# One written-out order of pieces replaced by another on all five queues of a vision tower kernel

## What is computed

```python
h = tok(x)                     # depthwise 3x3 convolution, 8x8 mean pooling: 64 tokens an image
h = h + attn0(layernorm(h))    # one head, 128 wide; values are the normalised tokens themselves
h = h + moe(layernorm(h))      # 2 shared experts, and the best 2 of 8 routed ones; hidden width 512
h = h + attn1(layernorm(h))    # 8 heads, rotary; 64 own keys, 15 compressed keys and a sink
h = h + mlp(layernorm(h))      # two 128x128 lower-triangular products with a gelu between
```

## Time and profile before

| | |
|---|---|
| time, median of three runs | 1983.51 us |
| the profiled execution's own time | 2000.31 us |
| its span, first to last instruction | 1998.4 us |
| TensorE busy | 1700.6 us, 85% |
| VectorE busy | 1307.9 us, 65% |
| ScalarE busy | 1070.4 us, 54% |
| GpSimd busy | 754.4 us, 38% |
| mean granted TensorE clock | 0.932 of full |
| moved by transfers | 331.56 MB, 166 GB/s |

### The profile page before, as it was taken

The page is one execution under the profiler, slowest core; times in us unless marked ns, Lnnn a source line. Parts: engine busy times, 40 slices in busy tenths (PEclk is TensorE's granted clock), DMA queues, the critical chain, the costliest instruction groups (busy, mean ns, idle before and its releaser), DMA issues.

```text
span 1998.4 us, 42920 instructions
## 1 busy us (share of the span) xinstructions
PE 1700.6 (85%) x14896; PEld 1320.4 (66%) x14896; DVE 1307.9 (65%) x3244; ACT 1070.4 (54%) x2707; POOL 754.4 (38%) x643
## 2 busy tenths in 40 slices
PE   1453888989998989999899999898999999897947
PEld 1443666867677777778676777777776768575624
DVE  2467476878677777568686777777777868442222
ACT  0122545647474747466564747474757566553532
POOL 1324244352536263344525263626353434213020
PEclk9999989999899999799998999999999999988775
DMA  6547455555655554445555555555455543101000
GB/s 253 223 172 261 164 209 194 184 176 183 219 182 176 202 203 173 153 174 191 181 187 206 183 196 205 176 186 206 163 208 185 203 164 147 43 15 53 12 22 6
DMA packets 109125, 331.56 MB, mean 166 GB/s; under 512 B 13662, under 2 KB 87585, under 8 KB 92412
## 3 DMA queue, kind: packets, MB, share of 16 engines
q1 hardware_dynamic: 86416, 300.90, 41.5%
q0 software_dynamic: 8992, 19.42, 3.0%
q10 hardware_dynamic: 13516, 8.50, 1.4%
HBM read 299.48 MB, written 29.29 MB: 165 GB/s over the span
## 4 chain that ended last, share of the span: by engine, by line
PE 42%; POOL 19%; DVE 14%; issue 13%; ACT 6%; DMA 4%; ACTq 1%; another core or an unknown queue 0%; SPq 0%; POOLq 0%; DVEq 0%
PE hid_bank L595 7%; POOL yg L1374 7%; PE sec_bank L649 5%; POOL rows_d L1352 5%; PE pool_bank L449 3%; POOL xbuf L1363 3%; PE sec_bank L669 3%; PE sec_bank L660 3%; PE hid_bank L580 3%; PE hid_bank L579 3%; PE pool_bank L454 2%; DVE xc L1268 2%; POOL rs L1335 2%; DVE x L1055 2%; PE hid_bank L581 2%
## 5 line engine op out<-in xcount | busy, mean ns | idle before, releaser
L1363 POOL TENSOR_TENSOR xbuf<-xbuf 128x512 f32<-128x512 f32 x256 | 328.2, 1282 | 633.0 <-DVE xbuf L1063 621.7
L845 ACT ACTIVATE hid<-hid_bank,bias_t 128x128 f32<-128x128 f32 x960 | 273.1, 371 | 116.0 <-PE hid_bank L581 113.6
L595 PE MATMUL hid_bank<-w_s,hid 128*128 x1920 | 291.2, 297 | 0.0
L595 PEld LDWEIGHTS hid_bank<-w_s,hid 128*128 128x128 f32 x1920 | 244.4, 199 | 16.9
L1084 DVE SCALAR_TENSOR_TENSOR taps<-pooled_s,tapw,taps 128x256 f32<-128x256 f32 (+1 forms) x416 | 240.5, 578 | 10.6
L1063 DVE TENSOR_TENSOR xbuf<-xbuf 128x1536 f32<-128x1536 f32 x128 | 224.0, 1750 | 30.4 <-DMA xbuf<-in_x 30.3
L579 PE MATMUL hid_bank<-xt,w_b 128*128 128x128 bf16 x960 | 213.2, 234 | 35.0 <-issue 17.1
L580 PE MATMUL hid_bank<-xt,w_b 128*128 128x128 bf16 x960 | 213.5, 234 | 0.7
L581 PE MATMUL hid_bank<-xt,w_b 128*128 128x128 bf16 x960 | 209.5, 230 | 0.0
L1374 POOL DMA_INDIRECT yg<-outs_d,spot_i x128 | 151.2, 1182 | 54.7 <-issue 38.8
L1067 DVE TENSOR_TENSOR xbuf<-xbuf 128x512 bf16<-128x512 f32 x128 | 102.1, 797 | 98.4 <-ACT xbuf L759 94.6
(11 more groups left out here) (215 smaller groups left out, 3464.8 us busy)
## 6 DMA issues: line engine op xcount, KB each, us to landing
xbuf<-in_x SPq DMA_DIRECT2D x128, 2048.0 KB
rows_s<-rows_d SPq DMA_DIRECT2D x48, 320.0 KB, 3.4
outs_d<-ys SPq DMA_DIRECT2D x240, 64.0 KB, 7.1
out<-h ACTq DMA_DIRECT2D x16, 256.0 KB
w_s<-in_w ACTq DMA_DIRECT2D x1, 2560.0 KB
hid<-in_w POOLq DMA_DIRECT2D x10, 256.0 KB, 3.4
rows_d<-x2r,spot_i POOLq DMA_INDIRECT x128
yg<-outs_d,spot_i POOLq DMA_INDIRECT x128
```

Of the source, the lines that this page charges most:

```text
L595: mm = nc.tensor.matmul(hid_bank[n % 2][:, 0:P], hid[:, n % RING, q * P:(q + 1) * P], w_q, start=False, stop=q == FC - 1)
L845: ins = nc.scalar.activation(hid[:, n % RING, cols], hid_bank[n % 2][:, cols], ACT.Gelu, bias=bias_t[:, q, j:j + 1])
L1363: nc.gpsimd.tensor_tensor(v[:, :, 1, :], v[:, :, 1, :], v[:, :, 2 * k + 3, :], ALU.add) \
```

## The change

Only the table `ORDER` changes. Every list keeps its words; they stand in another order, and for `dve`, `sp` and `pool` some pieces at the seam between two iterations move across it, which the mark `'` shows. No instruction is added or taken away, and no wait is.

```diff
     sp="""
-        store.6' store.7' store.4' store.9' store.10' store.8' load.0.0 store.13' store.11' store.12' store.14'
-        load.0.1 rows.1 rows.0 load.1.0 load.1.1 store.1 rows.2 load.2.0 store.0 store.2 load.2.1 store.3
-        load.3.0 load.3.1 store.5 keep.0""",
+        store.9' store.5' store.7' store.11' store.8' load.0.0 store.12' store.10' store.13' load.0.1 store.14'
+        rows.0 rows.1 load.1.0 rows.2 load.1.1 load.2.0 store.1 load.2.1 store.0 store.3 store.4 store.6 load.3.0
+        store.2 load.3.1 keep.0""",
     pe="""
-        up.0 up.1 table up.2 up.3 down.0 down.1 down.2 up.4 down.3 up.5 out' up.6 down.4 down.5 up.7 pool.0.0
-        pool.0.1 down.6 down.7 pool.0.2 lift.0 att.1 lift.1 widen.0 lift.2 widen.1 att.2 narrow.0 lift.3 pool.0.3
-        lift.4 widen.2 pre.2 narrow.1 pre.3 lift.5 att.3 lift.6 narrow.2 pre.4 att.4 pre.5 pre.6 lift.7 pre.7
-        widen.3 pool.1.0 pool.1.1 widen.4 pool.1.2 score.0 score.1 att.7 score.2 score.3 narrow.3 score.4
-        pool.1.3 score.5 widen.5 narrow.4 score.6 score.7 lift.8 att.8 widen.6 narrow.5 turn.0 widen.7 turn.1
-        pool.2.0 lift.9 value.0 pool.2.1 narrow.6 turn.2 lift.10 pool.2.2 att.10 widen.8 value.1 turn.3 value.2
-        narrow.7 turn.4 pool.2.3 value.3 lift.11 widen.9 turn.5 value.4 narrow.8 turn.6 value.5 att.11 widen.10
-        turn.7 lift.12 narrow.9 value.6 narrow.10 value.7 widen.11 att.12 lift.13 post.0 widen.12 pool.3.0 post.1
-        narrow.11 pool.3.1 pool.3.2 narrow.12 lift.14 widen.13 widen.14 pool.3.3 narrow.13 post.3 narrow.14
-        post.4 post.5""",
+        up.0 table up.1 down.0 up.2 up.3 down.1 up.4 up.5 down.2 up.6 down.3 up.7 out' down.4 down.5 down.6
+        down.7 pool.0.0 lift.0 pool.0.1 widen.0 lift.1 att.1 pool.0.2 lift.2 widen.1 lift.3 att.2 pool.0.3
+        narrow.0 att.3 pre.2 widen.2 lift.4 narrow.1 pre.3 widen.3 narrow.2 att.4 pre.4 narrow.3 pre.5 pre.6
+        widen.4 lift.5 pool.1.0 pre.7 pool.1.1 pool.1.2 score.0 score.1 lift.6 att.7 widen.5 score.2 score.3
+        narrow.4 score.4 widen.6 score.5 score.6 pool.1.3 lift.7 score.7 narrow.5 narrow.6 att.8 turn.0 lift.8
+        widen.7 turn.1 value.0 lift.9 widen.8 turn.2 value.1 pool.2.0 turn.3 pool.2.1 value.2 att.10 pool.2.2
+        lift.10 turn.4 narrow.7 value.3 att.11 turn.5 lift.11 widen.9 value.4 turn.6 lift.12 value.5 pool.2.3
+        narrow.8 turn.7 narrow.9 widen.10 value.6 att.12 widen.11 narrow.10 lift.13 value.7 widen.12 post.0
+        narrow.11 lift.14 post.1 pool.3.0 widen.13 narrow.12 pool.3.1 pool.3.2 widen.14 pool.3.3 narrow.13
+        narrow.14 post.3 post.4 post.5""",
     act="""
-        hidden.0 hidden.1 table hidden.2 hidden.3 inner.0.0 hidden.4 out' hidden.5 hidden.6 hidden.7 pool.0.0
-        inner.0.1 lift.0 pool.0.2 lift.1 att.1 widen.0 lift.2 widen.1 lift.3 narrow.0 att.2 pool.0.3 lift.4 pre.2
-        widen.2 lift.5 narrow.1 att.3 lift.6 gate narrow.2 pre.5 inner.1.0 pre.6 pre.7 split att.6 widen.3
-        inner.1.1 pool.1.0 pool.1.2 widen.4 narrow.3 att.7 pool.1.3 lift.7 widen.5 narrow.4 exp lift.8 narrow.5
-        inner.2.0 turn.0 widen.6 lift.9 turn.1 narrow.6 turn.2 widen.7 high att.10 lift.10 inner.2.1 turn.3
-        pool.2.0 pool.2.2 narrow.7 widen.8 turn.4 turn.5 widen.9 pool.2.3 narrow.8 turn.6 lift.11 widen.10 turn.7
-        narrow.9 inner.3.0 lift.12 narrow.10 widen.11 post.0 widen.12 narrow.11 pool.3.0 lift.13 pool.3.2
...
+        table hidden.0 hidden.1 hidden.2 hidden.3 hidden.4 hidden.5 hidden.6 inner.0.0 out' hidden.7 inner.0.1
+        lift.0 lift.1 att.1 pool.0.0 lift.2 widen.0 att.2 pool.0.2 lift.3 widen.1 att.3 narrow.0 pre.2 narrow.1
+        lift.4 widen.2 widen.3 gate pool.0.3 narrow.2 inner.1.0 pre.5 pre.6 split pre.7 narrow.3 lift.5 att.6
+        widen.4 widen.5 lift.6 pool.1.0 att.7 inner.1.1 narrow.4 widen.6 exp pool.1.2 narrow.5 lift.7 narrow.6
+        pool.1.3 turn.0 lift.8 inner.2.0 turn.1 widen.7 turn.2 lift.9 pool.2.0 turn.3 widen.8 att.10 turn.4
+        narrow.7 inner.2.1 lift.10 turn.5 lift.11 high widen.9 turn.6 narrow.8 narrow.9 lift.12 widen.10 turn.7
+        inner.3.0 widen.11 narrow.10 pool.2.2 lift.13 pool.2.3 post.0 widen.12 narrow.11 lift.14 widen.13
...
     dve="""
-        tap.1.9' pair.0.0 tap.1.10' tap.1.11' tap.1.12' tap.1.13' tap.1.14' inner.0.0 pair.0.1 att.0 att.1 moe
-        mix pre.1 inner.0.1 pre.2 pair.1.0 pre.5 pre.3 pre.4 att.4 inner.1.0 att.5 pair.1.1 score.0 score.1
-        score.2 inner.1.1 score.3 att.7 gate score.4 score.5 pair.2.0 score.6 score.7 att.8 att.9 inner.2.0
-        tap.0.0 att.10 pair.2.1 tap.0.1 tap.0.2 value.0 tap.0.3 tap.0.4 tap.0.5 value.1 inner.2.1 value.2 tap.0.6
-        tap.0.7 tap.0.8 low tap.0.9 value.3 tap.0.10 tap.0.11 tap.0.12 value.4 pair.3.0 value.5 att.11 value.6
-        inner.3.0 rest value.7 pair.3.1 att.12 post.1 post.2 inner.3.1 post.3 tap.0.13 tap.0.14 tap.1.0 tap.1.1
...
+        tap.1.8' pair.0.0 tap.1.9' tap.1.10' tap.1.11' tap.1.12' tap.1.13' tap.1.14' inner.0.0 pair.0.1 att.0 moe
+        att.1 mix inner.0.1 pre.1 pre.2 pre.5 pair.1.0 pre.3 att.4 pre.4 att.5 inner.1.0 pair.1.1 score.0 score.1
+        score.2 score.3 inner.1.1 score.4 att.7 gate score.5 score.6 score.7 pair.2.0 att.8 att.9 value.0 tap.0.0
+        inner.2.0 att.10 tap.0.1 value.1 pair.2.1 tap.0.2 tap.0.3 value.2 value.3 tap.0.4 att.11 value.4
+        inner.2.1 tap.0.5 low tap.0.6 rest value.5 tap.0.7 pair.3.0 value.6 att.12 value.7 tap.0.8 inner.3.0
+        pair.3.1 tap.0.9 post.1 post.2 tap.0.10 inner.3.1 tap.0.11 post.3 tap.0.12 tap.0.13 tap.0.14 tap.1.0
...
     pool="""
-        scatter.7' gather.0 gather.1 gather.2 add.0.0 add.0.1 gather.3 gather.4 gather.5 gather.6 gather.7 att.0
-        add.0.2 add.0.3 pre.1 pre.3 add.1.0 add.1.1 pre.4 add.1.2 add.1.3 add.2.0 add.2.1 att.9 add.2.2 add.2.3
-        add.3.0 add.3.1 add.3.2 add.3.3 scatter.0 scatter.1 post.1 post.2 scatter.2 scatter.3 scatter.4 scatter.5
-        scatter.6 weights.0 weights.1 weights.2 weights.3 weights.4 weights.5 weights.6 weights.7 weights.8
-        weights.9""")
+        scatter.5' scatter.6' scatter.7' gather.0 gather.1 gather.2 gather.3 gather.4 add.0.0 add.0.1 gather.5
+        gather.6 gather.7 add.0.2 add.0.3 att.0 pre.1 add.1.0 pre.3 add.1.1 pre.4 add.1.2 add.1.3 add.2.0 add.2.1
+        att.9 add.2.2 add.2.3 add.3.0 add.3.1 scatter.0 scatter.1 scatter.2 add.3.2 add.3.3 scatter.3 post.1
+        post.2 scatter.4 weights.0 weights.1 weights.2 weights.3 weights.4 weights.5 weights.6 weights.7
+        weights.8 weights.9""")
```

More of the change, by code:

```diff
@@ L83 @@
-    dve="""
-        tap.1.9' pair.0.0 tap.1.10' tap.1.11' tap.1.12' tap.1.13' tap.1.14' inner.0.0 pair.0.1 att.0 att.1 moe
-        mix pre.1 inner.0.1 pre.2 pair.1.0 pre.5 pre.3 pre.4 att.4 inner.1.0 att.5 pair.1.1 score.0 score.1
-        score.2 inner.1.1 score.3 att.7 gate score.4 score.5 pair.2.0 score.6 score.7 att.8 att.9 inner.2.0
-        tap.0.0 att.10 pair.2.1 tap.0.1 tap.0.2 value.0 tap.0.3 tap.0.4 tap.0.5 value.1 inner.2.1 value.2 tap.0.6
-        tap.0.7 tap.0.8 low tap.0.9 value.3 tap.0.10 tap.0.11 tap.0.12 value.4 pair.3.0 value.5 att.11 value.6
-        inner.3.0 rest value.7 pair.3.1 att.12 post.1 post.2 inner.3.1 post.3 tap.0.13 tap.0.14 tap.1.0 tap.1.1
-        tap.1.2 tap.1.3 tap.1.4 tap.1.5 tap.1.6 tap.1.7 post.5 tap.1.8 weights.0 weights.1 weights.2 weights.3
+        up.0 table up.1 down.0 up.2 up.3 down.1 up.4 up.5 down.2 up.6 down.3 up.7 out' down.4 down.5 down.6
@@ new lines @@
+        lift.10 turn.4 narrow.7 value.3 att.11 turn.5 lift.11 widen.9 value.4 turn.6 lift.12 value.5 pool.2.3
+        narrow.8 turn.7 narrow.9 widen.10 value.6 att.12 widen.11 narrow.10 lift.13 value.7 widen.12 post.0
+        narrow.11 lift.14 post.1 pool.3.0 widen.13 narrow.12 pool.3.1 pool.3.2 widen.14 pool.3.3 narrow.13
+        narrow.14 post.3 post.4 post.5""",
+    act="""
+        table hidden.0 hidden.1 hidden.2 hidden.3 hidden.4 hidden.5 hidden.6 inner.0.0 out' hidden.7 inner.0.1
[5 more added lines that the diff above has]
+        inner.3.0 widen.11 narrow.10 pool.2.2 lift.13 pool.2.3 post.0 widen.12 narrow.11 lift.14 widen.13
+        inner.3.1 narrow.12 pool.3.0 widen.14 narrow.13 narrow.14 pool.3.2 pool.3.3 post.3 post.4 post.5
+        weights.0 weights.1 weights.2 weights.3 weights.4 weights.5 weights.6 weights.7 weights.8 weights.9""",
@@ new lines @@
+    dve="""
+        tap.1.8' pair.0.0 tap.1.9' tap.1.10' tap.1.11' tap.1.12' tap.1.13' tap.1.14' inner.0.0 pair.0.1 att.0 moe
[4 more added lines that the diff above has]
+        pair.3.1 tap.0.9 post.1 post.2 tap.0.10 inner.3.1 tap.0.11 post.3 tap.0.12 tap.0.13 tap.0.14 tap.1.0
+        tap.1.1 tap.1.2 tap.1.3 tap.1.4 tap.1.5 post.5 tap.1.6 tap.1.7 weights.0 weights.1 weights.2 weights.3
```

2 lines of the change are left out of this document (removed).

## The result

The changed kernel takes **2324.57 us**, the median of four runs (2315.26 to 2328.64), beside 1976.32 for the kernel before (four runs, 1963.71 to 1990.41). The ratio is **1.1753, interval 1.1656 to 1.185**. The prediction was 2116 us, 2040 to 2168: the sign was right, the size was not. The profiled execution took 2323.79 us, its span is 2321.9. Some executions of a kernel lie over 1.5% above its fastest, e8's profiled one among them (2071.86 us beside 2036.13 and 2055.43); the medians given here take them in, the ratios leave them out.

A forecast was written before the change was run, and what follows sets the result against it. The prediction took TensorE, busy 85% of the span, as the bound. 95 + 17 - 4 + 25 = +133 us on the profiled 2000.3 gave 2133; less 16.8, that execution's excess over the median, 2116 us, range 2040 to 2168.

The forecast's parts named there:

- Part 1: SyncE's store.0 and store.2 land late behind loads; TensorE waits 3.5 us at lift.8, 3.3 at lift.11, fourteen times: +95 us.
- the lower bound's case: lift.8 and lift.11 find ScalarE late anyway and the stretch runs at the lower clock; half is hidden, +48 us.
- The sign that the prediction named: ScalarE's line 855 waits for stores some 28 times, about 100 us in all; iterations 2 to 15 near 116 us.
- Part 2: An iteration's first twenty microseconds: store.14 behind load.0.1 delays gathers and adds; waits at down.7, lift.0, widen.0; +17 us.
- Part 3: The seam between iterations: down.0 waits for hidden.0 where up.2 did, smaller waits are covered; -4 us.
- Part 4: TensorE's clock: one short low stretch behind each new wait, 39 us, less 14 us won back; +25 us.
- Rival D: The clock falls for long: a mid-iteration wait starts a 14 us stretch in every second iteration; 2194 us, 6%.
- The price of 3.4 us: Length at half clock of the short stretch expected behind each of the two new waits, 1.4 us lost each.

The follow-up runs named there:

- e8: e5 with three gathers before the first adds on GpSimd, and ScalarE's inner.0.0 and inner.0.1 moved; 2063.64 us, ratio 1.0245.
- e7: e5 with store.2 put back behind load.3.0, as in the changed kernel; 2167.68 us, ratio 1.0858.
- e5: The changed kernel with store.0 and store.2 ahead of load.2.1 and store.14 ahead of load.0.1; 2102.45 us, ratio 1.0512.
- e6: e5 with store.0 put back behind load.2.1, as in the changed kernel; 2230.79 us, ratio 1.1169.
- e2: The kernel before with the changed SyncE list alone; 2116.46 us, ratio 1.0726.

## Why the direction was right and the size wrong

**Part 1 (two late stores, +95 us): the mechanism held, half of the waiting came.** SyncE's queue, the landing of 7 us, the wait at `lift.8` (3.5 forecast, 3.55 seen) and the one at `lift.11` (3.3 forecast, 3.2 an iteration in e7) are as worked out. In after itself `lift.11` waits only in four of the thirteen iterations (4, 7, 9 and 14; 4.43 above), those in which `lift.8` waited for less than 1 us. In the others TensorE comes so late to it, at half clock, that ScalarE is ready: the lower bound's case, for one of the two. And in those four `lift.8` is itself hidden behind the low stretch of `score.0`. In the thirteen iterations `lift.8` waits 38 us and `lift.11` 14, together 51, where the forecast's 6.8 an iteration make 88. The sign that the prediction named came nearly as stated, line 855 waiting for transfers 31 times, 112 us in all (some 28 and 100); but its iterations of 116 us took 130 to 136.

**Part 2 (the first twenty microseconds, +17) was too small, by the landing.** It took 7.1 us from the earlier trace rows for `store.14`. The store landed 10.4 us after its issue there, the load 10.9 after its own. `gather.0` began 7.2 us into the iteration, the first adds 13.2. ScalarE's `inner.0.0` waited 6.71 us for them, with `hidden.7` behind it, and `down.7` waited 4.53 us where 1.0 was forecast; then next to nothing was left for `lift.0`, forecast at 1.3. Over the thirteen iterations `down.7` waits 55 us more than before, the products of line 579 (`widen`) 23 more and `lift.0` 21 less: 57 where 16 had been forecast. GpSimd's timeline:

```profile
987.93 0.98 POOL L1374 DMA_INDIRECT yg<-outs_d,spot_i  x1 [9.58 <-DMA outs_d<-ys]
...
993.93 2.62 POOL L1363 TENSOR_TENSOR xbuf<-xbuf 128x512 f32<-128x512 f32 x2
```

**One wait was overlooked:** `score.0`, 1.35 us an iteration, which no part of the sum names, 15 us more than before.

**Part 3 (the seam, -4)** is small either way: `post.5` waits 0.78 where it was about 1.2, and `post.4` has a new wait of 1.18; with the wait of `up.2` gone the seam has 7 us less in all.

Forecast were +108 us of idle time (95 + 17 - 4) and +111 came, but that is luck: part 1 was 37 us too large, part 2 41 too small, and `score.0` was not in it.

**Part 4 (the clock, +25) is the step that failed.** It said that behind each of the two new waits stands "one short stretch", 3.4 us at half clock. The price was nearly right: 25 us at 0.82 is a deficit of 30 us, and what came is 0.20 x 1722 less 0.05 x 1403, 274 us, for 208 of busy time, 0.76 each. The amount was nine times too small. The stretches last 3.4 to 34.1 us, three or four an iteration. In the profile of after they go with all thirteen waits of `down.7` (10 to 20 us each, once only at `widen.0` behind it), all thirteen of `score.0` (3.4 to 23.9), the nine of `lift.8` above 2.8 us and the four of `lift.11` (13.7); three more begin soon after such a stretch has ended. The 1.18 us at `post.4` has none. Rival D named that mechanism, but with one stretch of 14 us in every second iteration.

The price of 3.4 us had been read behind waits of the same length at `lift.0`, where before had stretches of 3.4 to 6.8 us. What the forecast lacked is that the place matters, and the rows hinted at it: most of the 13.9 us of busy time that one iteration lost in the earlier trace rows is one stretch of 27.31 us among `turn`, `value` and `pool` pieces. These are the windows ahead of it and of it, in before:

```profile
786.00:794.45 8.45, 8.31 (x96) 7.41 (x96) 7.96 (x25) 6.80 (x13) 3.21 (x4) 1.00 0.22 87
794.45:821.76 27.31, 27.31 (x209) 24.50 (x208) 13.63 (x41) 12.14 (x34) 4.43 (x4) 0.50 0.45 165
```

TensorE was idle for 0.14 us of the 8.45 ahead of the fall and for none of the 27.31 behind it. So a stretch among these pieces can also begin without a wait; a wait is one way into it, and both new waits of part 1 come among these pieces.

The page "TensorE: Matmul & The Clock Gate" of the Trainium skill (Terms) books the whole deficit as the penalty. By that rule the loss would be 274 us; the trace has 208 of busy time more. Why it is less than the rule gives is not shown. The same page (Part 1, "What's actually happening") puts the ramp penalty below 1% of a typical kernel span, speaking of the start of a kernel. The lower clock takes 9% here, 208 of 2322 us, since it comes back several times an iteration.

**What the change is worth, piece by piece.** From e5 up, the steps of the ratio are `store.0` late +6.6 points, `store.2` late +3.5, `store.14` late +2.7. From e5 down they are 2.7 for the order of gathers, adds and `inner`, 1.8 for the chain ahead of the scores and 0.3 for the end of the iteration; 0.3 are left. Together 17.9, beside the 17.5 measured. Most of these steps are differences along one row of kernels and add up by themselves; what the agreement tests is that the two stores in the middle cost the same one by one (6.6 and 3.5) as together (9.8). The loss is so traced to the order of these few pieces. The single steps below e5 are known less well (1.8 and 2.7 hang on e8, whose ratio has an interval of two points) than their sum, 4.8.

**Open:** why 3.2 us of waiting at `lift.8` bring 84 us of busy time and the same at `lift.11` 30. In e6 `lift.8` waits 2.3 us or more in nine iterations, and the stretch behind it, among `widen.7`, `turn` and `value` pieces, lasts 17 to 34 us; in the other four a stretch of 23.9 us behind `score.0` comes first. In e7 `lift.11` waits in all thirteen and its stretch lasts 13.65 us each time; it begins while TensorE still waits. In e2 waits of 4.6 to 9.2 us ahead of `up.6`, `down` and the first `pool` pieces have stretches of 3.4 to 6.8. One of e6, one of e7:

```profile
1514.85:1548.98 34.13, 33.82 (x255) 30.31 (x256) 15.56 (x45) 13.30 (x32) 5.27 (x4) 0.50 0.30 109
```
```profile
1236.33:1249.98 13.65, 11.36 (x86) 9.70 (x87) 6.41 (x18) 4.46 (x12) 2.54 (x2) 0.50 0.23 81
```

So the length of the wait alone does not decide. That the following pieces prolong the stretch is argued from this and not shown: no run changed them alone.

## What to carry to other kernels

Don't book a new wait of the bounding engine at its length alone: in these runs it cost 1.5 times that at `lift.11` and three times at `lift.8`. Read how long the lower clock stays in windows with the same pieces as those behind the new wait, not behind waits of the same length elsewhere. In a queue, put the small transfer that somebody waits for ahead of the large one, and look along the chain for the one engine whose next piece isn't needed and stands in front of one that is. An order that loses 17% may be an order with a handful of waits: mend each by moving a few words, and only then judge the idea.
